# Two transformer layers on one core: the totals of a softmax pair one step earlier, two ACT/POOL places moved, row maxima turned by a product

## The reference

```python
# layer 0                                  # layer 1
h = ada_norm(x, cond, ln1)                 h = ln(x) * (1 + sc1) + sh1
q, k, v = h@wq+bq, h@wk+bk, h@wv+bv        q = h@wq.T (16 heads); k, v: 4 heads
q, k = rotary(q), rotary(k)
a = softmax(q@k.T / sqrt(32))              a = softmax(q@k.T / sqrt(32))
x = x + (a@v)@wo + bo                      x = x + g1 * ((a@v)@wo.T)
h = ada_norm(x, cond, ln2)                 h = ln(x) * (1 + sc2) + sh2
x = x + gelu(h@w1+b1)@w2 + b2              x = x + g2 * (gelu(h@w1.T+b1)@w2.T + b2)
```

## Time and profile before

| | |
|---|---|
| time, median of 3 runs | 3954.84 us (3951.35 to 3958.53) |
| the profiled execution | 3957.61 us, span 3955.8 us |
| mean granted TensorE clock | 0.980 |
| PE busy | 3746.3 us (95%) |
| DVE busy | 2471.2 us (62%) |
| POOL busy | 1613.5 us (41%) |
| ACT busy | 1603.8 us (41%) |
| HBM | 223.46 MB read, 36.66 MB written |

### The profile page before, as it was taken

One profiled execution on the slowest core, in us unless ns is written; L12 is line 12 of the kernel. 1 busy time (PEld: TensorE's weight loads), 2 busy tenths in 40 slices (PEclk: granted clock), 3 DMA queues, 4 the chain that ended last, 5 costly groups with the idle time before them and its releaser, 6 DMA issues.

```text
span 3955.8 us, 76367 instructions
## 1 busy us (share of the span) xinstructions
PE 3746.3 (95%) x31828; PEld 1559.4 (39%) x31828; DVE 2471.2 (62%) x3951; ACT 1603.8 (41%) x2807; POOL 1613.5 (41%) x907
## 2 busy tenths in 40 slices
PE   7988999999998989999899999999999999999999
PEld 4422444333543335433354333433344333543344
DVE  5677735766457755467654777467664776467752
ACT  1466313554125642155521663136621563126621
POOL 2467212672216742066510672137520672126611
PEclk8899999999999999999999999999999999999999
DMA  5233243212423123431232112311123112311122
GB/s 153 48 99 119 85 107 81 72 55 84 109 76 87 41 91 91 106 75 53 100 101 83 34 42 89 115 44 29 65 96 98 31 40 81 114 54 26 63 67 96
DMA packets 139110, 306.67 MB, mean 78 GB/s; under 512 B 19680, under 2 KB 59636, under 8 KB 137872
## 3 DMA queue, kind: packets, MB, share of 16 engines
q10 hardware_dynamic: 50944, 174.62, 13.6%
q1 hardware_dynamic: 87824, 127.17, 12.1%
HBM read 223.46 MB, written 36.66 MB: 66 GB/s over the span
## 4 chain that ended last, share of the span: by engine, by line
PE 79%; DVE 7%; POOL 5%; issue 4%; ACT 3%; DMA 1%; ACTq 0%; SPq 0%; POOLq 0%; DVEq 0%
PE ps L931 15%; PE ps L834 12%; PE ps L835 12%; PE ps L836 12%; PE ps L1029 9%; PE ps L871 7%; PE ps L1044 5%; PE ps L888 3%; POOL sums L730 3%; ACT probs L1209 3%; DVE mcol L1532 2%; PE ps L947 2%; PE ps L852 1%; DVE ring L1582 1%; DVE turn L1466 1%
## 5 line engine op out<-in xcount | busy, mean ns | idle before, releaser
L1532 DVE TENSOR_REDUCE mcol<-ps 128x1 f32<-128x512 f32 x2048 | 1290.0, 683 | 441.2 <-PE ps L931 226.7
L730 POOL TENSOR_TENSOR sums<-probs 128x1024 f32<-128x1024 f32 x448 | 1065.2, 2392 | 943.0 <-PE ps L1044 510.9
L1209 ACT ACTIVATE probs<-ps 128x512 f32<-128x512 f32 x2048 | 1098.8, 608 | 812.0 <-PE ps L931 564.3
L931 PE MATMUL ps<-qs,ks 98*32 98x512 f16 x8192 | 800.6, 389 | 105.4 <-ACT probs L1209 93.5
L931 PE MATMUL ps<-ks,qs 97*32 97x512 f16 x7040 | 697.3, 385 | 53.7 <-DVE mcol L1532 41.5
L1355 ACT ACTIVATE sums<-ps,cols 128x512 f32<-128x512 f32 x256 | 175.8, 687 | 1097.0 <-PE ps L836 1097.0
L1029 PE MATMUL ps<-probs,v_sb 128*32 128x512 f32 x4096 | 548.5, 612 | 0.0
L931 PEld LDWEIGHTS ps<-qs,ks 98*32 98x32 f16 x8192 | 215.5, 97 | 589.9 <-ACT probs L1209 363.9
L834 PE MATMUL ps<-ring,probs 128*128 128x512 f16 x1024 | 388.0, 379 | 0.3 <-DVE probs L1627 0.3
L834 PE MATMUL ps<-aT,ring 128*128 128x512 f16 x1024 | 388.1, 379 | 0.0
L836 PE MATMUL ps<-aT,ring 128*128 128x512 f16 x1024 | 388.0, 379 | 0.0
(11 more groups left out here) (112 smaller groups left out, 3471.9 us busy)
## 6 DMA issues: line engine op xcount, KB each, us to landing
ring<-halves ACTq DMA_DIRECT2D x208, 512.0 KB, 3.3
qs<-hl SPq DMA_DIRECT2D x192, 128.0 KB, 4.1
ring<-halves SPq DMA_DIRECT2D x48, 512.0 KB, 6.2
ring<-in_weights ACTq DMA_DIRECT2D x39, 512.0 KB, 4.6
halves<-ring ACTq DMA_DIRECT2D x37, 512.0 KB, 2.9
ks<-hl SPq DMA_DIRECT2D x120, 128.0 KB, 4.4
dcopy<-inverses SPq DMA_DIRECT2D x56, 256.0 KB
probs<-in_x SPq DMA_DIRECT2D x8, 1024.0 KB, 8.3
```

The lines of the kernel that those rows point to most:

```text
L730: pool.tensor_tensor(sums[:, m % SUM_SLOTS, :, :], prob(u - 2), prob(u), ALU.add).then_inc(sum_set[0].sem, 1)
L931: mm = pe.matmul(bank[cut, :], lhs[:, cut], rhs, start=True, stop=True)
L1209: act.activation(prob(u)[:, e, :], ps[:, w % SCORE_BANKS, :], ACT.Exp).then_inc(exp_done.sem, 1)
L1532: dve.tensor_reduce(mcol[:, blk % 2, 4 * j + qt, half:half + 1], src, AX.X, ALU.max).then_inc(n_free[0], 1)
```

## The change

Three edits. The totals of a pair are computed in step `2p + 3` in all items, where it was `2p + 4` but for the first two pairs in layer 0; the last two pairs of an item keep their steps. The high half of a block's output is written by ACT at place 15 and no longer 11, the low half by POOL behind sum 3 and no longer 1. The rows of maxima are made by a plain product with the identity as the moving operand and no longer by a transpose.

```diff
-O_AT, D_AT, HI_AT, INVERT_AT, NORM_AT, LO_AT = 7, 12, 11, 4, 6, 1
+O_AT, D_AT, HI_AT, INVERT_AT, NORM_AT, LO_AT = 7, 12, 15, 4, 6, 3
...
     if pair >= SUMS // 2 - 2:
         return STEPS - 1 if pair == SUMS // 2 - 2 else STEPS + 1
-    return 2 * pair + (3 if layer(i) == 0 and pair < 2 else 4)
+    return 2 * pair + 3
...
-                pe.transpose(bank[0:16, 0:P], mfin[:, :], ident[:, :]).then_inc(n_full, 1)
+                pe.matmul(bank[0:16, 0:P], mfin[:, :], ident[:, :], start=True, stop=True).then_inc(n_full, 1)
```

## The result

The changed kernel takes 3862.39 us (median of 4 runs, 3856.33 to 3869.38) where the kernel before took 3955.41 on the same chip: ratio 0.9766, 95% interval 0.9747 to 0.9785, a gain of 93 us. The profiled execution took 3856.33 us, with a span of 3854.5.

A forecast was written before the change was run, and what follows sets the result against it. PE was taken to lead, held back by short stalls. Gains of 24 us in layer 1 and 28 in layer 0, less 3, made 49 off 3957.6: 3908.6, with the median 2.8 lower, so 3906 us; range 3862 to 3962.

The forecast's parts named there:

- The circle: In attention steps, POOL's sums wait for PE's totals, ACT for those sums, PE for ACT; POOL's 510.9 us falls under 150.
- The waits put down to the values: ACT's 84.7 us of waits named for the values (L1029): many of these 99 waits are really for POOL's sum.
- rival "no change": ACT isn't freed, as the 84.7 us are truly for the values and POOL's slack is used up: 3950 to 3960, chance 0.08.
- The steady block and the new stall: Layer 1 block falls from 26.17 to 25.2 us: 1.7 gained, less about 0.7 of PE waiting for the maxima's fold.
- Layer 0, 28 us: Attention of layer 0: 7 us gained an item, 28 for four, from 6.9 us of PE's idle time and what idle time hides.
- "Less half for DVE": Layer 0: DVE, busy 192.44 of 288.00 us, binds some blocks too, so half is taken off the regained time.
- rival "more": PE gets all stalls back and the clock, 0.96 in item 1, rises toward 0.99: 3860 us, chance 0.17.
- The product, -3 us: Rows of maxima by product: 0.11 us dearer, 7 us over 64, bounds 0 and 19; 3 us loss added to the sum.
- Places, 0: Copies of the output's halves at places 15 and 3: the two keep step with each other, so 0 us.
- The unknown, L1582: DVE's low halves in layer 0, 74 taking 96.3 us: may gain up to 45 or lose up to 105; range takes 20 each way.
- The SP side: Between rows of maxima and next block's first score, 0.86 us more room for mT's DMA: 1 to 3 us gain, left in range.
- The slower rival: PE waits for ACT's d_copy at a block's first totals once its 0.87 us of room is used up: 3980 us, chance 0.12.

The follow-up runs named there:

- the fourth slot: Kernel before with a fourth slot for POOL's sums in layer 1 (rotary table's free half), totals left at 2p+4: 3911.62 us, ratio 0.9897.
- its own change alone: Kernel before with totals at 2p+3 in one block of each item only: last block 3930.92 us (0.9941), third block 3930.20 us (0.9934).

## Why the prediction was right in kind and off in size

- *The circle.* Right. POOL's waits for L1044 are 99.1 us (under 150 was said), ACT's for POOL's sums 12.6 (under 40), and the fourth slot removed the circle with no totals moved.
- *The waits put down to the values.* Right: 84.7 us before, 3.7 after, which also settles the rival "no change".
- *The steady block and the new stall.* Right: 25.3 us after where 25.2 was said, with 0.68 us of stall at L977 where 0.67 was said. Layer 1 gave 25 us for 24, in part by luck. In item 5 the three steady blocks gave 2.7 us (3.0 was said), the three with other products between 2.1 (0.6 was said), and the two ends 0.8 (2.4 was said).
- *Layer 0, 28 us.* The term that was mis-sized: it measured 53 with the totals alone, the edit for which it was worked out, and 74 in the profile of the whole change. The step that failed reads: "There ACT waits 6.4 us for DVE's own sums, which stand behind the normalising work in DVE's order and stay." By it 8.5 us of PE's idle time in this block were taken off the sum. ACT's waits do mostly stay (5.0 us after), but PE's idle time fell to 3.5: the longest stall hung on a wait of the normalising work, 6.64 us, for POOL, and POOL had waited for the totals. The last block gave 6.8 us in item 1 and 5.7 by its own change alone, against nothing forecast. The working followed the wait one engine back and stopped at DVE's order.
- *"Less half for DVE".* The halving was wrong as well. The third block, in which DVE is busy 30.21 of 35.40 us, gave 5.1 us, and 4.1 by its own change alone.
- *The clock.* It stood among the reasons of the rival "more", with chance 0.17, though the window of item 1 showed 0.96 and item 5 0.99. That rival's 3860 is what came, partly by luck: its terms add 34 us for layer 1 (25 came) and 80 for layer 0 (74 came), which is 114 and not 115, and then take off 20 for the rows. In the last block the stall and the low clock come together, so a forecast that removes such a stall should have taken part of the clock in its sum.
- *The product, -3 us.* Not borne out: alone it lies between 4 us faster and 2 us slower (0.9989 to 1.0006 of 3954), and L977 holds PE no longer than the transpose does in the same place. The Trainium skill's Perfetto Trace Analysis, Transposes, prefers the transpose; at 16 x 128 no run here shows a difference in time, so at this size the measurement doesn't bear its advice out.
- *Places, 0.* Wrong: about 10 us faster with the new totals, and 36 us slower by themselves. The prediction asked whether the copies' inputs were there in time, and not what stands behind the copy on ACT.
- *The unknown, L1582.* It went the good way and is small; no run shows what of it reached the end. The groups by line of the kernel after:

```profile
L1582 DVE SCALAR_TENSOR_TENSOR ring<-ring 128x512 f16<-128x512 f32 x74 | 85.7, 1160 | 0.3 <-ACT ring L1235 0.3
```

That is 10.6 us less than in the earlier trace rows.
- *The SP side.* The waits for the DMA of `mT` fell from 18.5 us (14.3 of weight loads, 4.2 of matmuls) to 12.2 (8.8 and 3.4), a little more than the 1 to 3 us left in the range.
- *The slower rival.* PE isn't seen to wait for `d_copy` in the waits of the kernel after; the 0.87 us of room held, and nothing of it came.

## What to carry to other kernels

When a wait looks as if it stays because another engine's own order holds it, follow that order back until something that is not late is found; here it led from ACT over DVE's sums, its normalising and POOL's deviation to the very wait that was removed. A copy is free or dear by what its engine would do in that time, so the place of a copy is judged again whenever a stall near it goes: the same two numbers cost 36 us with one schedule and gained 10 with the other. Where a product is moved from behind a wait, look for what it had covered, and move the covered thing too: this was worth another 25 us by the medians, 15 by the profiled executions.

## What the runs showed of the hardware

A plain fp32 product with the identity (two matmuls, 16 x 128) cost no time that was seen over the transpose of one matmul: 0.9998 (0.9989 to 1.0006), and 0.24 us from L977 to the next product with either.

After PE had been busy for 0.39 us of 3.06, its granted clock stood at 0.50 for the next 6 us, in which it was busy 2.32 and then 3.06 of 3.06 us. It also fell without any idle time of PE: within 2 us behind 32 products of 4 columns that took 3.74 us, to 0.50.
